# Attention and feed-forward pipeline: the sums of squares moved behind the rotary product, and half of a token shift copied by ScalarE

## The chip, the cores and the metric

The kernel runs on one core of a Trainium2 chip. The metric is the device time of one execution in microseconds (us). The program is static: each engine (TensorE = PE, VectorE = DVE, ScalarE = ACT, GpSimd = POOL) and the DMA-issuing SyncE (SP) has its own instruction list, runs it strictly in order, and meets the others only in semaphores.

## What is computed

The input is x of shape (2, 1024, 128). The output is x + attention(layernorm(x)) + f(layernorm(x)). The first part, 16 causal heads of 8 channels, is not touched by the change. The second part, f, is six layers of:

```
x = attn_layer(shift_tokens(x), ...) + x
x = ffn_layer(shift_tokens(x), ...) + x

def shift_tokens(t):                      # first 64 channels stay, last 64 come from the token before
    a, s = split(t, 2, -1)
    return concatenate([a, pad(s, one row ahead)[:, :-1]], -1)

attn_layer: q, k, v = split(x @ Wqkv)     # 16 heads of 64 channels
    q = q / max(norm(q), 1e-12) * q_scale;  k likewise
    q = q * cos * scale + rotate_half(q) * sin * scale;  k likewise with 1/scale
    windows of 32 queries see 64 keys; softmax(8 * q k^T); out @ Wo
ffn_layer: layernorm(x) * g + b;  a, gate = split(. @ W1 + b1);  (a * gelu(gate)) @ W2 + b2
```

All is float32 in the second part.

## The kernel before

The second part works on tiles of 128 tokens: 6 layers x 16 tiles = 96 tiles (`n_tiles`). It is a software pipeline of 108 steps. In step s each engine runs its share of several tiles at once, in an order written out by hand (loops at L597 for PE, L820 for DVE, L1023 for ACT, L1168 for POOL, L1332 for SP). The feed-forward part handles groups of four tiles and lies 10 steps behind (`FF = 10`). In the text "stage k" is a step s with (s - 10) % 4 = k: normalisation and the two large feed-forward products are started in stage 3, the down product follows in stage 0, the residual and the statistics in stage 1.

For tile n the work is:

- PE `project` (L488) makes q and k (m = 0 and 1) into PSUM, two pairs of banks. ACT `project` (L954) copies both halves into `qk_raw`; ACT squares the copies (L960) into the single buffer `qk_sq`.
- DVE `norms` (L735) sums the squares of 64 channels per head. ACT `roots` (L942 to L946) and POOL `norms` (L1122 to L1130) make the reciprocal norm from it, with one Newton step on POOL.
- DVE `rotate` (L784) multiplies the projection in PSUM with the cosine table into `qk_rot`, one instruction for q and one for k; it waits for ACT's raw copy of the same half. Each releases a pair of PSUM banks (semaphore `rc`). POOL `rotate` makes the sine product out of `qk_raw` (L1151, four instructions) and adds it (L1159, two).
- Two to three steps later DVE `scale` (L743, two instructions) multiplies by the reciprocal norm. PE `turn` (L497) transposes k and q, ACT `turn` copies them out (L967 to L974), PE `score` (L505, L515) makes the window scores, DVE `subtract` (L770 maximum, L774 subtraction) takes the maximum away, ACT `exponents` (L983) exponentiates, DVE `sums` (L757, L759) and `normalise` (L763) divide, PE `weights_turn` (L536) and ACT `weights` (L988) transpose the weights, PE `gather` (L555), ACT `outputs` (L993), PE `output` (L565), DVE `residual` (L752) end the tile. V goes by PE L528, ACT L979, and through DRAM by SP (L1304, L1315).

PSUM is four pairs of banks used in turn; `place` walks the order of use, and each use waits until the reader of the use four places earlier is done. In a step without feed-forward work the order is scores, q, k, output, gather, turned k, turned q, v, turned weights. So turned k of tile s-3 waits for `rotate` of q of tile s, turned q for `rotate` of k of tile s, the gather pair for `subtract`; in stage 3 one more place (normed x turned) makes v wait for ACT `outputs`. The three pairs of the up product (L582), read by `ff_gate` (L806), are reused by q, k and output of the next stage 0.

The engines' orders in one step are:

- PE: score(s-4), project(s), output(s-6), gather(s-5), turn(s-3), [stage 3: L572], project_v(s-2), weights_turn(s-4), [stage 1: shift_in L477], [stage 0: ff_down L592], [stage 3: ff_up L582]
- DVE: scale(s-3), subtract(s-4), [stage 1: ff_residual L817], norms(s-1), rotate(s), residual(s-6), sums and normalise(s-4), [stage 1: ff_stats L796, L798], [stage 3: scale(s-2), which the next step then leaves out, and ff_gate L806]
- ACT: [stage 3: ff_norm L1000], exponents(s-4), project(s) with roots(s-1) and the squares inside it, outputs(s-5), turn(s-3), [stage 3: ff_gain L1008], values(s-2), weights(s-4), [stage 1: shift_in L934, L935], [stage 3: gelu L1018 between two table loads]
- POOL: rotate(s-1), [now and then tables L1085, L1093 and a clearing L1165], [stage 2: ff_rsqrt L1136 to L1141], norms(s-1)

The feed-forward part's own token shift is made by SP in `shift_rows` (L1325 to L1330) in stage 0: three DMAs from `X` to `Xs` (the unshifted 64 channels, 128 KB; the shifted ones, 127 KB; one row), and for the first half of a sequence one more row. `ff_stats` waits for three DMAs of 16 counts each.

Waits are written with `Once`, which leaves out a wait that an earlier one of the same engine covers.

## Time and profile before

| | |
|---|---|
| median of 3 runs | 2046.61 us (2038.38 to 2047.28) |
| the profiled execution, its own time | 2042.86 us |
| span of the profile | 2041.0 us |
| granted TensorE clock, mean | 0.957 of full |
| busy: PE, DVE, ACT, POOL | 92%, 81%, 67%, 68% |
| second part's first projection | at 355 us |
| stage 0 of the first feed-forward group, of the last | at 478 us and 1911.56 us |

The busy share of PE is that of an engine whose matrix products are pipelined and whose ends are modelled. A bracket after a row of the timeline is idle time ahead of it, with the engine and line that released it; "issue" is idle time for which the profile shows no releaser. Times in the timeline are from the start of the span. Durations of POOL are rough; the distance from one start to the next is the better measure.

### The profile page before, as it was taken

To read this page: it belongs to the slowest core of one execution; us is meant where nothing else is said; L and a number is where in the kernel's file an instruction comes from. 1 tells how busy PE (TensorE), PEld (TensorE's weight loads), DVE (VectorE), ACT (ScalarE), POOL (GpSimd) and SP (SyncE) were. 2 spreads that over 40 slices of the span, in tenths; PEclk is the share of its full clock that TensorE was granted. 3 is DMA by queue.
4 is the path that set the end of the run, shared out by engine and by line. 5 is a ranking of instruction groups with operands and counts; after the bars stand their busy time and mean duration, and the time that the engine had idled before them with its cause. 6 is when DMAs were issued, how large, how long until landed. Compare 5 with 4: busy or idle time off the path is not lost.

```text
span 2041.0 us, 73638 instructions
## 1 busy us (share of the span) xinstructions
PE 1872.9 (92%) x32776; PEld 1259.4 (62%) x32776; DVE 1657.3 (81%) x1819; ACT 1373.1 (67%) x2014; POOL 1395.5 (68%) x1277
## 2 busy tenths in 40 slices
PE   3989997889899999999999999999999999999995
PEld 1434443467666766676666676767666766676674
DVE  5777771799798888988888988899878988998872
ACT  1356566677776777776667776777667767777753
POOL 1011112899987889786877788878778878887820
PEclk7689999899999999998999999999999999999997
DMA  3141100254343434444333444344343443333331
GB/s 105 32 142 55 47 25 22 75 134 117 81 120 103 122 101 124 113 116 111 95 107 107 122 115 113 97 112 125 108 112 91 132 121 108 100 96 98 100 101 47
DMA packets 139805, 201.72 MB, mean 99 GB/s; under 512 B 44249, under 2 KB 69085, under 8 KB 138721
## 3 DMA queue, kind: packets, MB, share of 16 engines
q1 hardware_dynamic: 139488, 197.02, 35.0%
q8 instruction: 258, 4.23, 0.9%
q14 instruction: 59, 0.48, 0.1%
HBM read 134.84 MB, written 55.77 MB: 93 GB/s over the span
## 4 chain that ended last, share of the span: by engine, by line
PE 54%; DVE 23%; issue 11%; ACT 6%; POOL 4%; DMA 1%; SPq 0%; DVEq 0%; POOLq 0%; ACTq 0%
PE banks L488 8%; PE banks L582 6%; PE banks L497 5%; PE banks L528 5%; PE banks L515 5%; PE banks L555 4%; PE banks L565 4%; DVE arena L646 4%; DVE ss L735 3%; PE banks L425 3%; PE banks L592 3%; DVE arena L784 3%; PE banks L536 3%; DVE mx_t L770 3%; DVE arena L743 2%
## 5 line engine op out<-in xcount | busy, mean ns | idle before, releaser
L1151 POOL TENSOR_TENSOR arena<-arena,tab_sl 128x512 f32<-128x512 f32 x384 | 600.1, 1594 | 15.7 <-ACT arena L954 8.2
L1159 POOL TENSOR_TENSOR arena<-arena 128x1024 f32<-128x1024 f32 x192 | 493.9, 2593 | 0.0
L743 DVE TENSOR_TENSOR arena<-arena,rn 128x1024 f32<-128x1024 f32 x192 | 379.6, 2017 | 6.8 <-POOL rn L1130 6.4
L488 PE MATMUL banks<-w_qkv,arena 128*128 128x512 f32 x768 | 359.9, 612 | 9.0 <-ACT arena L935 6.6
L983 ACT ACTIVATE arena<-arena 128x1024 f32<-128x1024 f32 x96 | 101.5, 1057 | 360.6 <-DVE arena L774 360.6
L784 DVE TENSOR_TENSOR arena<-banks,tab_cl 128x1024 f32<-128x1024 f32 x192 | 226.2, 1219 | 21.1 <-ACT arena L954 19.3
L488 PEld LDWEIGHTS banks<-w_qkv,arena 128*128 128x128 f32 x768 | 140.2, 192 | 160.9 <-issue 151.4
L646 DVE TENSOR_REDUCE arena<-banks 128x1 f32<-128x512 f32 (+3 forms) x352 | 183.6, 587 | 67.2 <-PE banks L385 55.9
L497 PE MATMUL banks<-ident,arena 128*128 128x128 f32 x1536 | 209.2, 292 | 29.5 <-DVE arena L784 21.3
L1101 POOL TENSOR_SCALAR_AFFINE_SELECT arena<-arena 128x512 f32<-128x512 f32 x64 | 40.9, 640 | 268.6 <-ACT arena L892 268.4
L892 ACT ACTIVATE arena<-banks 128x512 f32<-128x512 f32 (+2 forms) x352 | 156.6, 529 | 101.1 <-PE banks L407 90.8
L735 DVE TENSOR_REDUCE ss<-arena 128x32 f32<-128x2048 f32 x96 | 218.5, 2276 | 1.3 <-ACT arena L960 1.3
L555 PE MATMUL banks<-arena 64*64 64x32 f32 x12288 | 202.5, 220 | 16.6 <-issue 15.2
L565 PEld LDWEIGHTS banks<-w_o,arena 128*128 128x128 f32 x1536 | 189.0, 194 | 45.0 <-issue 33.3
L555 PEld LDWEIGHTS banks<-arena 64*64 64x64 f32 x12288 | 190.6, 135 | 30.7 <-issue 17.4
L497 PEld LDWEIGHTS banks<-ident,arena 128*128 128x128 f32 x1536 | 181.7, 150 | 39.5 <-DVE arena L784 26.8
L528 PE MATMUL banks<-w_qkv,arena 128*128 128x512 f32 x384 | 187.2, 610 | 9.4 <-DVE arena L784 5.5
L954 ACT COPY arena<-banks 128x1024 f32<-128x1024 f32 x192 | 183.9, 1009 | 12.0 <-PE banks L488 7.1
L565 PE MATMUL banks<-w_o,arena 128*128 128x128 f32 x1536 | 190.7, 278 | 1.1 <-ACT arena L993 1.1
L960 ACT ACTIVATE arena<-arena 128x1024 f32<-128x1024 f32 x192 | 191.2, 1044 | 0.0
L770 DVE TENSOR_REDUCE mx_t<-banks 128x16 f32<-128x1024 f32 x96 | 116.7, 1216 | 82.5 <-PE banks L515 82.5
L515 PE MATMUL banks<-arena 64*32 64x64 f32 x12288 | 146.5, 226 | 13.5 <-issue 13.5
(111 smaller groups left out, 3002.9 us busy)
## 6 DMA issues: line engine op xcount, KB each, us to landing
arena<-v_dram SPq DMA_DIRECT2D x360, 256.0 KB, 4.7
v_dram<-arena SPq DMA_DIRECT2D x96, 512.0 KB, 3.1
arena<-parts_dram SPq DMA_DIRECT2D x64, 144.0 KB
w_qkv<-Wqkv SPq DMA_DIRECT2D x6, 1024.0 KB, 5.0
arena<-v_dram SPq DMA_DIRECT2D x24, 192.0 KB, 3.4
parts_dram<-arena SPq DMA_DIRECT2D x12, 256.0 KB, 3.0
tab_cl<-tab_c SPq DMA_DIRECT2D x6, 512.0 KB, 7.7
tab_sl<-tab_s SPq DMA_DIRECT2D x6, 512.0 KB, 10.6
```

The lines of the kernel that those rows point to most:

```text
L488: last = e.matmul(ps[:, BANK * c:BANK * (c + 1)], xsT[b][:, P * t:P * (t + 1)], w_qkv[:, at:at + BANK], start=True, stop=True)
L497: last = e.transpose(ps[:, P * c:P * (c + 1)], qk_rot[n % 4][:, m, P * c:P * (c + 1)], ident)
L515: last = e.matmul(ps[WINDOW * i:WINDOW * (i + 1), col:col + 2 * WINDOW], QT[r, c, WINDOW * i:WINDOW * (i + 1)], KT[n % 2][r, c, WINDOW * i ...
L528: last = e.matmul(ps[:, BANK * hp:BANK * (hp + 1)], xsT[b][:, P * t:P * (t + 1)], w_v[:, hp], start=True, stop=True)
L555: last = e.matmul(ps[d:d + HEAD_DIM, at:at + WINDOW], Vw[n % 3][r, i, P * c + d:P * c + d + HEAD_DIM], PT[r, CHUNKS // 2 * half + c, q], s ...
L565: last = e.matmul(ps[:, 0:P], OT[:, c % 2 * (CHUNKS // 2) + c // 2, :], w_o[l % 2][:, c, :], start=c == 0, stop=c == CHUNKS - 1)
L646: e.tensor_reduce(to, banks[:, pair_of["a_sc", k], BANK * bank:BANK * (bank + 1)].rearrange("p (j n) -> p j n", j=heads.stop - heads.start ...
L735: e.tensor_reduce(ss[n % 4][:, :], qk_sq.rearrange("p m (h d) -> p (m h) d", d=HEAD_DIM), AX_X, ALU.add).then_inc(S["ss_sum"], 1)
L743: e.tensor_tensor(to, to, rn[n % 4][:, HEADS * m:HEADS * (m + 1)].unsqueeze(2).to_broadcast([P, HEADS, HEAD_DIM]), ALU.mult).then_inc(S["r ...
L784: e.tensor_tensor(qk_rot[n % 4][:, m, :].rearrange("p (h d) -> p h d", d=HEAD_DIM), banks[:, pair_of["proj", n, m], :].rearrange("p (h d) ...
L1151: e.tensor_tensor(qk_sw[:, m, :].rearrange("p (h d) -> p h d", d=HEAD_DIM)[:, :, d:d + HALF], raw[:, m, :].rearrange("p (h d) -> p h d", d ...
L1159: e.tensor_tensor(to, to, qk_sw[:, m, :], ALU.add).then_inc(S["rs"], 1)
```

## The change

On DVE, `norms(s-1)` moves from before `rotate(s)` to behind `normalise(s-4)`. On ACT, `project` is split: the copy of q comes ahead of the exponentials; the copy of k stays behind them except in stage 2, where it is ahead too; roots and squares become `squares(s)` and move to the end of the step, ahead of gelu in stage 3. The DMA of the unshifted channels becomes a copy on ACT (`ff_left`, 128 x 256 elements) at the start of stage 0, with a semaphore of its own, and `ff_stats` waits for two DMAs and that copy.

```diff
@@ vector_program @@
             def ff_stats(G):
                 half = G % halves
-                w.wait_ge(xf_in[half], 48 * (G // halves + 1))
+                w.wait_ge(xf_in[half], 32 * (G // halves + 1))
+                w.wait_ge(S["xf_left"], G + 1)
...
-                if 0 <= s - 1 < n_tiles:
-                    norms(s - 1)
                 if s < n_tiles:
                     rotate(s)
...
                     sums(s - 4)
                     normalise(s - 4)
+                if 0 <= s - 1 < n_tiles:
+                    norms(s - 1)
                 if ff_here and k == 1:
                     ff_stats(G)
@@ scalar_program @@
-            def project(n):
-                raw = qk_raw[n % 2]
-                for m in range(2):
-                    w.wait_ge(S["proj"], 2 * n + m + 1)
-                    if n >= 2:
-                        w.wait_ge(S["sw"], 4 * (n - 1))
-                    e.copy(raw[:, m, :], banks[:, pair_of["proj", n, m], :]).then_inc(S["raw"], 1)
+            def project(n, m):
+                w.wait_ge(S["proj"], 2 * n + m + 1)
+                if n >= 2:
+                    w.wait_ge(S["sw"], 4 * (n - 1))
+                e.copy(qk_raw[n % 2][:, m, :], banks[:, pair_of["proj", n, m], :]).then_inc(S["raw"], 1)
+
+            def squares(n):
                 w.wait_ge(S["ss_sum"], n)
                 if n:
                     roots(n - 1)
...
+            def ff_left(G):
+                l, b, half = of_group(G)
+                w.wait_ge(S["x_attn"], GROUP * (G + 1))
+                w.wait_ge(S["xf_norm"], max(0, GROUP * (G - halves + 1)))
+                e.copy(Xs[half][:, :, 0:HEAD_DIM], X[:, b * tiles + half * GROUP:b * tiles + (half + 1) * GROUP, 0:HEAD_DIM]
+                       ).then_inc(S["xf_left"], 1)
...
+                if ff_here and k == 0:
+                    ff_left(G)
                 if ff_here and k == 3:
                     ff_norm(G)
+                if s < n_tiles:
+                    project(s, 0)
+                if s < n_tiles and s >= FF and k == 2:
+                    project(s, 1)
                 if 0 <= s - 4 < n_tiles:
                     exponents(s - 4)
-                if s < n_tiles:
-                    project(s)
-                if s == n_tiles:
-                    roots(s - 1)
+                if s < n_tiles and not (s >= FF and k == 2):
+                    project(s, 1)
...
                     shift_in((s + 1) // GROUP)
+                if s < n_tiles:
+                    squares(s)
+                if s == n_tiles:
+                    roots(s - 1)
                 if ff_here and k == 3:
                     ff_gelu(G)
@@ sync_program, shift_rows @@
-                e.dma_start(to[:, :, 0:HEAD_DIM], xg[:, :, 0:HEAD_DIM]).then_inc(xf_in[half], 16)
```

## Rows read from the trace of the kernel before

**Rows 1.** Busy time by stretch: start:end, length, busy us by engine, clock, DMA share, GB/s
```profile
477.79:1911.56 1433.77, 1371.68 (x26947) 982.00 (x26941) 1257.56 (x1176) 1043.22 (x1428) 1192.95 (x1058) 0.98 0.41 110
```
**Rows 2.** The same columns, stages 0, 1, 2, 3 of one group
```profile
1643.43:1659.75 16.32, 16.32 (x340) 12.80 (x335) 14.16 (x12) 11.28 (x15) 10.14 (x11) 1.00 0.40 104
1659.75:1674.30 14.55, 14.34 (x319) 10.46 (x315) 14.10 (x20) 11.54 (x16) 11.65 (x12) 1.00 0.62 184
1674.30:1690.07 15.77, 14.14 (x311) 9.95 (x311) 15.60 (x12) 10.27 (x14) 13.32 (x14) 1.00 0.31 70
1690.07:1710.21 20.14, 19.73 (x333) 12.58 (x327) 16.70 (x15) 16.36 (x25) 19.53 (x15) 1.00 0.50 140
```
**Rows 3.** Timeline of PE, stages 2 and 3: start us, us, engine line op
```profile
1683.22 2.22 PE L497 MATMUL banks<-ident,arena 128*128 128x128 f32 x16 [1.42 <-DVE arena L784]
...
1700.28 1.98 PE L528 MATMUL banks<-w_qkv,arena 128*128 128x512 f32 x4 [0.39 <-ACT arena L993]
```
**Rows 4.** Waits from 500 to 2000 us: us in total, times, longest
```profile
PE banks L497 <- DVE arena L784: 21.3, 15, 4.6
```
**Rows 5.** Timeline of DVE, starts of stages 1, 2 and 3, and stage 2
```profile
1659.86 1.23 DVE L770 TENSOR_REDUCE mx_t<-banks 128x16 f32<-128x1024 f32 x1 [2.16 <-PE banks L515]
...
1677.21 1.21 DVE L770 TENSOR_REDUCE mx_t<-banks 128x16 f32<-128x1024 f32 x1
...
1679.60 2.27 DVE L735 TENSOR_REDUCE ss<-arena 128x32 f32<-128x2048 f32 x1
1681.94 2.36 DVE L784 TENSOR_TENSOR arena<-banks,tab_cl 128x1024 f32<-128x1024 f32 x2
...
1687.11 4.18 DVE L743 TENSOR_TENSOR arena<-arena,rn 128x1024 f32<-128x1024 f32 x2
1691.21 1.21 DVE L770 TENSOR_REDUCE mx_t<-banks 128x16 f32<-128x1024 f32 x1
```
**Rows 6.** Timeline of PE in an earlier group, stages 2, 3, 0
```profile
1206.04 0.42 PE L555 MATMUL banks<-arena 64*64 64x32 f32 x12 [2.10 <-issue]
...
1214.29 3.70 PE L488 MATMUL banks<-w_qkv,arena 128*128 128x512 f32 x8
...
1233.52 3.70 PE L488 MATMUL banks<-w_qkv,arena 128*128 128x512 f32 x8
...
1245.33 2.84 PE L592 MATMUL banks<-w,arena 128*128 128x128 f32 x24
```
**Rows 7.** Timeline of ACT, stage 3
```profile
1694.68 1.91 ACT L954 COPY arena<-banks 128x1024 f32<-128x1024 f32 x2
...
1697.33 2.00 ACT L960 ACTIVATE arena<-arena 128x1024 f32<-128x1024 f32 x2
...
1704.83 1.28 ACT L1018 ACT_TABLE_LOAD   x1
...
1713.15 1.06 ACT L983 ACTIVATE arena<-arena 128x1024 f32<-128x1024 f32 x1 [1.90 <-DVE arena L774]
```
**Rows 8.** Timeline of DVE, its first work of the next stage 0
```profile
1710.64 1.21 DVE L770 TENSOR_REDUCE mx_t<-banks 128x16 f32<-128x1024 f32 x1
```
**Rows 9.** Timeline of POOL, stages 2 and 3
```profile
1679.58 0.22 POOL L1136 TENSOR_SCALAR ln_v<-mean_var 128x4 f32<-128x4 f32 x1
...
1685.01 7.25 POOL L1151 TENSOR_TENSOR arena<-arena,tab_sl 128x512 f32<-128x512 f32 x4
1692.21 4.68 POOL L1159 TENSOR_TENSOR arena<-arena 128x1024 f32<-128x1024 f32 x2
```
**Rows 10.** Timeline of DVE and POOL past the last tile's rotation
```profile
1952.79 2.42 DVE L743 TENSOR_TENSOR arena<-arena,rn 128x1024 f32<-128x1024 f32 x2
...
1953.12 1.01 POOL L1130 TENSOR_TENSOR rn<-rn,rs_g 128x32 f32<-128x32 f32 x1
```
**Rows 11.** A copy of 128 x 256 on ACT, and the third DMA issue of the shift
```profile
1701.02 0.39 ACT L970 COPY arena<-banks 128x256 f32<-128x256 f32 x1
...
1706.41 8.02 SPq L1327 DMA_DIRECT2D arena<-X  x1
```

More of the change, by code:

```diff
@@ L102 @@
 sc mx sub v_proj v_ready v_out vw_first ex sm recip p_norm pT pt pv ot wo x_attn
-f_stat f_mv f_var f_rstd xf_norm f_nT xft h gel u_one u f_out x_ff final""".split()
+xf_left f_stat f_mv f_var f_rstd xf_norm f_nT xft h gel u_one u f_out x_ff final""".split()
 def build(nc, ins, out, scratch, parts_dram, rows_dram):
@@ L959, in project @@
                     w.wait_ge(S["raw"], 2 * n + m + 1)
-                    e.activation(qk_sq[:, m, :], raw[:, m, :], ACT.Square).then_inc(S["sq"], 1)
+                    e.activation(qk_sq[:, m, :], qk_raw[n % 2][:, m, :], ACT.Square).then_inc(S["sq"], 1)
             def turn(n):
```

## The prediction

> **What bounds the kernel now.** I read the busy time by stretch first. The steady stretch holds 21 feed-forward groups in 1433.8 us, 68.3 us each; PE is busy for 96% of it, DVE 88%, POOL 83%, ACT 73% [rows 1]. So PE is nearly the bound and only its remaining idle time can be won. The same view of one regular group, stage by stage, says where that is: 66.8 us in all, stage 2 being 15.8 us long with 14.1 us of PE [rows 2].
>
> What would PE need undisturbed? Stage 0 shows no wait: 16.3 us [rows 2], of which the down product is 2.8 [rows 6]; a stage without extras is therefore 13.5. Stage 3 without a wait takes 19.2 (the two starts of the projection in an earlier group, [rows 6]), stage 1 has four more transposes, 14.0. The sum, 16.3 + 14.0 + 13.5 + 19.2, is a floor of 63.1 us for a group, 3.7 under the regular one: 2.2 in stage 2, 0.9 in stage 3, 0.5 in stage 1.
>
> The timeline of PE names the waits: in stage 2 turned k waits 1.42 us for the rotary product of DVE, in stage 3 v waits 0.39 us for ACT's `outputs` [rows 3]. The first kind comes back 15 times, 21.3 us in all [rows 4]. The timeline of DVE shows why: it begins stage 2 at 1677.2, 2.9 us behind PE's projection (at 1674.3), because stage 1 took it 17.4 us (1659.9 to 1677.2) [rows 5]. Then the sum of squares runs for 2.3 us, though nobody needs it soon, ahead of the rotary product, which holds the PSUM banks that PE wants [rows 5]. So in stages 1 and 2 DVE ends the wait; in stage 3 the chain comes back through ACT and gelu.
>
> **The change, part by part.** *Sum of squares last on DVE.* No instruction is added or removed. Rotation of q is done 3.6 us after the maximum begins (1.25 + 1.15 for maximum and subtraction, 1.15 for the product) and not after 5.9. PE turns k 7.4 us after its projection began. Before, DVE could be 1.5 us late, now 3.8; the gather wants the subtraction after 5.4 us, and that allows 3.0. With the 2.9 us of stage 2 the whole 2.2 us of stage 2 goes, and the 0.5 of stage 1, whose turned weights come 2.3 us earlier. What is late next: the sum itself, now 9.9 us into DVE's step; ACT's roots wait for it only at the end of the step, after about 13 us. `scale` needs the norm two steps later, so this costs nothing while the roots are where they are.
>
> *Copy of q before the exponentials, squares last on ACT.* Roots and squares (0.8 + 1.9 us, from the end of the copies to the end of L960 [rows 7]) stood ahead of `outputs`; without them `outputs` starts at once when the gather ends, and the 0.9 us of stage 3 goes. Against it:
> (a) In stages 0, 1 and 3 the copy of k stays behind the exponentials. It is ready 1.06 + 0.95 us [rows 7] after the subtraction, but DVE is through with q after 1.15: a new wait of 0.9 us in three stages, 2.7 a group, that the sum of squares used to cover.
> (b) In stage 3 the 2.7 us now stand ahead of the table load. Gelu used to be ready for stage 0 to begin on DVE 5.8 us after the load began (1704.8 to 1710.6 [rows 7, 8]); DVE's stage 0 will now begin about 3 us after PE's projection and not 0.4. Maximum and subtraction are then done at 5.5 us (wanted 5.4), rotated k at 8.9 (8.3), weights at about 11.8 (10.9): about 0.8 us of PE waits in stage 0 and 0.3 in stage 3.
> ACT itself has room, 49.5 of 66.8 us busy [rows 2].
>
> *POOL.* The roots reach POOL some 9 us later in a step, so its norms and the next rotation move by as much. Its work is 54.6 of 66.8 us [rows 2], and its result is used two steps on, so nothing waits for the rotation. One thing may: `ff_rsqrt`, which ran at 1679.6, over 10 us before stage 3 began at 1690.1 [rows 9, 2]. One rotation is 7.2 + 4.7 us [rows 9]; put behind the later roots, it ends some 2.8 us into stage 3, while ACT would take `ff_norm` at 2.1. That holds the copy of q there by about 2.3 us, but DVE, itself late by then, loses only 0.3.
>
> *Does DVE become the bound?* Its loop, from the rows: stage 0 14.0, stage 1 17.4, stage 2 14.0 (1677.2 to 1691.2), stage 3 to the end of the sum 9.8, then roots and squares 2.7, and 5.8 from table load to stage 0 [rows 5, 7, 8]: 63.7, and 2.7 with (a): 66.4 us, hardly less than now. But `scale` is not one size. Beside POOL's large products its two instructions take 4.18 us [rows 5]; after the last rotation, beside small POOL work, they take 2.42, and a POOL instruction of a quarter of a us takes 1.01 beside them [rows 10]. The later roots leave POOL idle or in its small operations just when DVE scales in stages 0 and 1. I price this between 0 (same overlap) and 4 x 1.76 = 7.0 us a group (never beside a large product), and take two stages, 3.5 us: the loop is 62.9 and PE bounds again. I take the nearer value since POOL is still busy for 55 of 64 us and must overlap elsewhere.
> The Trainium skill (SBUF — State Buffer, Who interferes with whom) states that a DVE instruction with two SBUF inputs and a GpSimd one that reads SBUF exclude each other, the second one blocking fully; by it `scale` would pay for every large POOL product in progress and nothing beside a waiting POOL. It would make the sum depend on POOL's phase alone, as taken above, not on its busy share.
>
> *The DMA replaced.* Removed: 24 DMAs of 128 KB and their SP issues; the third issue of the shift, behind them, takes 8.0 us [rows 11], so SP may reach the V windows sooner, but these are wanted two steps later and no PE wait on them is seen. Added: 24 copies of 128 x 256 at 0.39 us [rows 11], 9 us of ACT. They lie after the second table load of stage 0, where ACT now idles 1.9 us before the exponentials [rows 7]; with gelu 2.7 us later that cover is gone for the copy of q, yet DVE's subtraction ends later still, so I cost it at 0; uncovered it would be 0.4 x 21 = 8 us. `ff_stats` needs the data some 25 us later: nothing. Behind the DMA, no gain either; bounds: 0, and the instruction stalls below if they come from DMA load.
>
> *Start and end.* In the first ten steps POOL's rotation sets the pace and is unchanged; in the last ten steps no projection is left. I take 0, between -5 and +5.
>
> *The sum.* A regular group becomes 17.1 (stage 0) + 14.0 + 13.5 + 19.5 = 64.2, that is 2.6 us less; 21 of them, 54 us. PE also has stalls with no releaser, such as 2.10 us within the gather [rows 6]; about 30 us in the stretch. Today half of that falls into time in which PE would wait for DVE anyway; it comes into the open and gives 15 us back. 2042.9 (the profiled execution's own time, 1.9 above its span and 3.7 under the median of the three runs) - 39 is 2003.9. Against the median that is 2007; I take 2004, as a faster run lies at 2038.
>
> **The rivals.** A difference of 0.5%, 10 us, is about what a measurement of this kernel can tell from no change.
> *Bigger gain.* `scale` is freed in all stages, so the new waits vanish too: the group comes to its floor, 3.7 x 21 = 77 us, about 1968. For it: the late POOL phase. Against: POOL's large products must lie somewhere. 0.15.
> *Nothing much.* The overlap stays as it is, and (a) replaces the sum of squares as what DVE stands on: 66.4 against 66.8 us, 8 us in all, 2036. For it: 4.18 us of `scale` in nearly every step today. 0.14. That the reorder doesn't free the banks I exclude: each rotation releases them itself.
> *Slower, by `ff_rsqrt`.* If POOL gets no relief, a rotation takes 13.9 and not 11.9, and `ff_norm`, first in ACT's stage 3, waits until 4.7 us into it. Copy of q, rotation, sum of squares, roots and gelu shift in a row, about 2 us on a loop of 66.4: 68.4 against 66.8, and 1.6 x 21 = 34 us, 2076 (2050 if half of it is absorbed). It decides from the point at which `ff_rsqrt` ends later than about 3 us into stage 3. Against it: today 10 us of room. 0.14.
> *The forecast*, 1985 to 2030: 0.57.
>
> **The numbers.** The range leaves out the far ends of the bigger gain and of the slower case: 1966 to 2052. Faster by over 0.5% is the forecast, the bigger gain and a small part of the third case: 0.73; within 0.5% 0.13; slower 0.14.
>
> **What would show it.** In the changed profile: the wait of L497 for DVE L784 near zero and stage 2 at 13.5 us; v in stage 3 without a wait; about 0.9 us of DVE idle time before the second L784 released by ACT's copy in stages 0, 1 and 3; gelu 2 to 3 us later; `scale` nearer 2.4 than 4.2 us in stages 0 and 1; POOL's wait for the roots now at the end of a step. Wrong would be: waits of L515 or L555 for DVE L774 or L784 of over 1 us a group, of ACT L1000 for POOL L1141, or stage 0 over 17.5 us.

## The result, and the profile after

| | before | after |
|---|---|---|
| median | 2039.95 us (6 runs, 2037.17 to 2047.28) | 2025.79 us (6 runs, 2020.29 to 2033.02) |
| profiled execution | 2042.86 us, span 2041.0 | 2033.02 us, span 2031.2 |
| first stage 0 of the feed-forward, last | 477.8, 1911.56 us | 484.21, 1900.63 us |
| 21 groups between them | 1433.8 us | 1416.4 us |

The ratio is 0.9933, 95% interval 0.9914 to 0.9952: faster by 0.67%, where 2.1% was forecast (2004 against the median of 2046.61 us known then). The range of 1966 to 2052 us holds it. The two spans differ by 9.8 us: 6.4 us lost before the first group, 17.4 us won in the steady stretch, 1.1 us lost behind it.

Busy time by stretch, after: stages 0 to 3 of one group, then all 21 groups (columns as in [rows 1]).
```profile
1495.89:1512.87 16.98, 16.73 (x341) 12.70 (x335) 13.49 (x13) 13.78 (x18) 8.06 (x8) 1.00 0.38 101
1512.87:1527.15 14.28, 14.14 (x320) 10.53 (x315) 13.30 (x18) 9.17 (x12) 12.30 (x8) 1.00 0.42 112
1527.15:1541.35 14.20, 13.82 (x311) 9.99 (x311) 14.10 (x13) 11.52 (x16) 13.42 (x12) 1.00 0.44 114
1541.35:1562.00 20.65, 19.70 (x331) 12.61 (x327) 16.48 (x14) 17.27 (x26) 19.59 (x21) 1.00 0.30 83
484.21:1900.63 1416.42, 1359.71 (x26946) 971.07 (x26940) 1186.60 (x1174) 1082.63 (x1450) 1097.42 (x1052) 0.99 0.40 109
```
Against [rows 2] stage 2 is 1.6 us shorter, but stage 0 is 0.7 us longer and stage 3 0.5: 66.1 us a group instead of 66.8, where 64.2 was forecast.

PE is busy for nearly all of this, and yet it is not what sets the 66.1 us. In another group of the changed kernel, stages 2 and 3 read:
```profile
985.93:1001.58 15.65, 14.05 (x310) 10.06 (x310) 15.55 (x14) 12.94 (x19) 14.79 (x13) 1.00 0.39 105
1001.58:1020.81 19.23, 19.23 (x328) 12.46 (x326) 15.12 (x13) 15.67 (x23) 18.25 (x20) 1.00 0.29 86
```
```profile
1001.39 0.27 PE L515 MATMUL banks<-arena 64*32 64x64 f32 x2 [1.22 <-issue]
```
A stall of PE (1.22 us idle, no releaser) makes stage 2 about 1.4 us longer here, stage 3 is shorter by as much, and the group takes 66.1 us again (16.98 + 14.28 + 15.65 + 19.23). Ten of the 21 groups lie between 66.10 and 66.24 us, however their stages are divided; they are called regular below, and undisturbed where PE has no stall either. Before, eight lie between 66.74 and 66.78 us. So a chain that runs through the other engines too sets the length, and it leaves PE about 1.4 us of slack in these two stages.

DVE and POOL are busy for 71 and 96 us less than in [rows 1]: that relief is real, but most of it doesn't reach PE. DVE's waits for ACT's copies, below, grow by 70 us.

The waits from 500 to 2000 us, after (us in total, times, longest), against [rows 4]:
```profile
POOL ss L1138 <- ACT rn L943: 277.0, 62, 9.0
DVE arena L784 <- ACT arena L953: 78.1, 86, 2.1
PE banks L536 <- DVE arena L763: 14.2, 22, 2.6
ACT arena L1008 <- POOL ln_m L1157: 12.9, 14, 2.8
PE banks L497 <- DVE arena L784: 1.1, 4, 0.3
```
The wait of turned k (L497) is gone, as forecast: 21.3 to 1.1 us. In its place stand more waits of DVE for ACT's copies (before: 7.7 us, 3 times), of PE for the normalised weights (before: 5.1 us, 14 times) and of ACT's `ff_norm` for POOL.

The timeline of DVE in stage 3, after (start us, us, engine line op; in brackets the idle time ahead):
```profile
1542.84 1.21 DVE L770 TENSOR_REDUCE mx_t<-banks 128x16 f32<-128x1024 f32 x1
1544.09 1.23 DVE L774 TENSOR_TENSOR arena<-banks,mx_t 128x1024 f32<-128x1024 f32 x1
1547.12 1.23 DVE L784 TENSOR_TENSOR arena<-banks,tab_cl 128x1024 f32<-128x1024 f32 x1 [1.80 <-ACT arena L953]
1548.87 1.23 DVE L784 TENSOR_TENSOR arena<-banks,tab_cl 128x1024 f32<-128x1024 f32 x1 [0.53 <-ACT arena L953]
...
1551.74 2.22 DVE L763 TENSOR_TENSOR arena<-arena,rs_o 128x1024 f32<-128x1024 f32 x1
1553.89 2.27 DVE L735 TENSOR_REDUCE ss<-arena 128x32 f32<-128x2048 f32 x1
```
What it waits for stands in ACT's timeline of the same stage:
```profile
1544.44 1.65 ACT L1008 ACTIVATE arena<-arena,ln_m,ln_r 128x128 f32<-128x128 f32 x4 [0.93 <-POOL ln_m L1157]
1546.00 0.99 ACT L953 COPY arena<-banks 128x1024 f32<-128x1024 f32 x1
```
and what follows, in PE's:
```profile
1554.11 1.07 PE L536 MATMUL banks<-ident,arena 128*128 128x128 f32 x8 [0.44 <-DVE arena L763]
```
`ff_norm` stands in ACT's list ahead of the copy of q, and waits for the last instruction of POOL's `ff_rsqrt`, which now follows a rotation that the later roots have shifted. The copy of q stands behind both that wait (0.93 us) and `ff_norm` itself (1.65 us):
```profile
1535.01 5.68 POOL L1175 TENSOR_TENSOR arena<-arena 128x1024 f32<-128x1024 f32 x2
...
1544.21 0.20 POOL L1157 TENSOR_TENSOR ln_m<-ln_m,ln_r 128x4 f32<-128x4 f32 x1
```
DVE stands still for 2.3 us (1.80 + 0.53), so sum, division and turned weights come late.

The groups of instructions of DVE and POOL from 500 to 1900 us (count | busy us, mean ns of one): first before, then after.
```profile
L743 DVE TENSOR_TENSOR arena<-arena,rn 128x1024 f32<-128x1024 f32 x164 | 329.5, 2049 | 0.2 <-issue 0.2
L763 DVE TENSOR_TENSOR arena<-arena,rs_o 128x1024 f32<-128x1024 f32 x82 | 116.0, 1415 | 2.8
L1151 POOL TENSOR_TENSOR arena<-arena,tab_sl 128x512 f32<-128x512 f32 x332 | 517.5, 1590 | 6.5
```
```profile
L743 DVE TENSOR_TENSOR arena<-arena,rn 128x1024 f32<-128x1024 f32 x167 | 199.9, 1236 | 0.0
L763 DVE TENSOR_TENSOR arena<-arena,rs_o 128x1024 f32<-128x1024 f32 x83 | 174.5, 2102 | 2.9
L1167 POOL TENSOR_TENSOR arena<-arena,tab_sl 128x512 f32<-128x512 f32 x334 | 357.9, 1104 | 6.6
```
`scale` (L743) costs 130 us less in all, more than the 3.5 x 21 = 74 us forecast, and POOL's sine products 160 us less. But `normalise` (L763), which lay clear of the large products and now lies beside POOL's addition, costs 58 us more, and that one stands directly ahead of PE's L536. This fits the rule of the Trainium skill weighed in the prediction (SBUF — State Buffer, Who interferes with whom): a DVE instruction with two SBUF inputs and a GpSimd one that reads SBUF exclude each other. The trace agrees: `scale` and `normalise` both have two SBUF inputs, and each is long where it lies beside one of POOL's products or additions. Below this is called the lock of the two engines.

### The profile page after: what moved, and what is told of

It reads as the page before. It is cut to its first block, busy times and chain, and to the rows that moved or that the text cites. A ratio compares the mean times of both kernels' runs of the same rounds, so it can differ in the third digit from the quotient of the medians.

```text
span 2031.2 us, 73684 instructions
## 1 busy us (share of the span) xinstructions
PE 1864.3 (92%) x32776; PEld 1253.0 (62%) x32776; DVE 1591.5 (78%) x1819; ACT 1415.4 (70%) x2038; POOL 1305.3 (64%) x1277
## 4 chain that ended last, share of the span: by engine, by line
PE 48%; DVE 21%; ACT 15%; issue 10%; POOL 5%; DMA 1%; SPq 0%; DVEq 0%; ACTq 0%; POOLq 0%
PE banks L488 8%; PE banks L497 5%; PE banks L555 4%; PE banks L582 4%; PE banks L528 4%; PE banks L565 4%; DVE arena L646 4%; PE banks L425 3%; DVE arena L763 3%; PE banks L592 3%; PE banks L515 3%; PE banks L536 3%; ACT arena L953 3%; DVE sm_t L757 3%; ACT arena L1026 2%
## 5 line engine op out<-in xcount | busy, mean ns | idle before, releaser
L1175 POOL TENSOR_TENSOR arena<-arena 128x1024 f32<-128x1024 f32 x192 | 499.1, 2624 | 0.0
L1167 POOL TENSOR_TENSOR arena<-arena,tab_sl 128x512 f32<-128x512 f32 x384 | 414.3, 1112 | 15.7 <-ACT arena L953 8.2
L784 DVE TENSOR_TENSOR arena<-banks,tab_cl 128x1024 f32<-128x1024 f32 x192 | 232.7, 1221 | 100.7 <-ACT arena L953 100.5
L1138 POOL TENSOR_SCALAR ss<-ss 128x32 f32<-128x32 f32 x96 | 69.2, 721 | 284.5 <-ACT rn L943 281.8
L743 DVE TENSOR_TENSOR arena<-arena,rn 128x1024 f32<-128x1024 f32 x192 | 244.1, 1311 | 0.0
L953 ACT COPY arena<-banks 128x1024 f32<-128x1024 f32 x192 | 192.0, 1004 | 63.7 <-PE banks L488 63.1
L497 PE MATMUL banks<-ident,arena 128*128 128x128 f32 x1536 | 209.7, 290 | 19.9 <-issue 12.6
L994 ACT COPY arena<-banks 128x1024 f32<-128x1024 f32 x96 | 97.4, 1015 | 156.6 <-PE banks L555 156.3
L763 DVE TENSOR_TENSOR arena<-arena,rs_o 128x1024 f32<-128x1024 f32 x96 | 198.4, 2067 | 3.3
L497 PEld LDWEIGHTS banks<-ident,arena 128*128 128x128 f32 x1536 | 178.6, 148 | 33.0 <-issue 19.9
L961 ACT ACTIVATE arena<-arena 128x1024 f32<-128x1024 f32 x192 | 190.9, 1042 | 0.0
```

The source lines that it names most:

```text
L497: last = e.transpose(ps[:, P * c:P * (c + 1)], qk_rot[n % 4][:, m, P * c:P * (c + 1)], ident)
L743: e.tensor_tensor(to, to, rn[n % 4][:, HEADS * m:HEADS * (m + 1)].unsqueeze(2).to_broadcast([P, HEADS, HEAD_DIM]), ALU.mult).then_inc(S["r ...
L763: e.tensor_tensor(PB, PB, rs_o[n % 2][:, :].unsqueeze(2).to_broadcast([P, HEADS, 2 * WINDOW]), ALU.mult).then_inc(S["p_norm"], 1)
L784: e.tensor_tensor(qk_rot[n % 4][:, m, :].rearrange("p (h d) -> p h d", d=HEAD_DIM), banks[:, pair_of["proj", n, m], :].rearrange("p (h d) ...
L953: e.copy(qk_raw[n % 2][:, m, :], banks[:, pair_of["proj", n, m], :]).then_inc(S["raw"], 1)
L1167: e.tensor_tensor(qk_sw[:, m, :].rearrange("p (h d) -> p h d", d=HEAD_DIM)[:, :, d:d + HALF], raw[:, m, :].rearrange("p (h d) -> p h d", d ...
```

## The experiments

All profiled runs are read alike; T is the start of the first stage 0, "steady" the 21 groups behind it, the stages are medians in us. Ratios are to the kernel before, measured together with the run. T, steady and the stages come from one profile each: before and e1 have the same regular groups (66.8 us), and their steady stretches still differ by 6 us. A difference of that size in this column is no finding; the length of the regular groups repeats to 0.1 us.

| run | ratio (95%) | T | steady | st. 0 | st. 1 | st. 2 | st. 3 |
|---|---|---|---|---|---|---|---|
| before | | 477.8 | 1433.8 | 16.32 | 14.55 | 15.77 | 20.14 |
| after | 0.9933 (0.9914-0.9952) | 484.2 | 1416.4 | 17.01 | 14.30 | 15.62 | 19.78 |
| e1 | 0.9976 (0.9960-0.9992) | 476.4 | 1427.8 | 16.32 | 14.55 | 15.77 | 20.14 |
| e2 | 0.9942 (0.9919-0.9966) | 484.6 | 1409.1 | 17.01 | 14.29 | 15.21 | 19.66 |
| e3 | 0.9947 (0.9928-0.9967) | 486.4 | 1417.8 | 17.01 | 14.29 | 14.83 | 20.21 |
| e4 | 0.9920 (0.9892-0.9948) | 477.5 | 1418.0 | 17.01 | 14.29 | 15.31 | 19.77 |
| e5 | 0.9896 (0.9848-0.9945) | 486.8 | 1402.0 | 16.43 | 14.29 | 15.97 | 19.79 |
| e6 | 1991.05 us, one run | 474.0 | 1387.7 | 16.98 | 14.28 | 14.66 | 19.23 |
| e7 | 0.9826 (0.9810-0.9843) | 479.4 | 1392.4 | 16.32 | 14.29 | 14.76 | 19.60 |
| e8 | 2025.54 us, one run | 472.5 | 1425.0 | 16.32 | 14.55 | 15.77 | 20.14 |
| e9 | 2010.43 us, one run | 480.4 | 1396.5 | 17.01 | 14.29 | 14.20 | 20.68 |
| e10 | 0.9880 (0.9859-0.9901) | 474.8 | 1404.8 | 16.43 | 14.29 | 15.65 | 19.89 |
| e13 | 1997.48 us, one run | 467.3 | 1401.2 | 16.32 | 14.55 | 15.22 | 19.79 |
| e14 | 0.9878 (0.9839-0.9917) | 481.6 | 1395.6 | 16.99 | 14.29 | 15.42 | 19.23 |
| e15 | 0.9771 (0.9732-0.9810) | 475.9 | 1377.4 | 16.32 | 14.29 | 14.26 | 19.23 |
| e16 | 0.9846 (0.9814-0.9879) | 480.5 | 1397.9 | 16.40 | 14.29 | 15.29 | 19.23 |

### The parts of the change, each alone

e1 is the kernel before with `ff_left` and its waits, and without the first DMA of the shift (the changed waits of `ff_stats` are as in the change):
```diff
+                if ff_here and k == 0:
+                    ff_left(G)
...
-                e.dma_start(to[:, :, 0:HEAD_DIM], xg[:, :, 0:HEAD_DIM]).then_inc(xf_in[half], 16)
```

> The kernel before with only the DMA of the unshifted channels replaced by the ScalarE copy; the orders of VectorE and ScalarE as before. Theory A (the copy and the DMA are both hidden; the result comes from the two orders alone): within 0.3% of the kernel before, stage 0 stays at 16.3 us, stage 2 at 15.8. Rival B (fewer small DMA packets relieve PE's instruction stalls): 0.3 to 0.8% faster, and idle time of PE before L555, L515 and L497 put down to issue falls from about 32 us to under 20. Rival C (the copy delays stage 0): stage 0 at 16.6 us or more, 0.3% slower.

e2 is the changed kernel with that DMA back:
```diff
-                w.wait_ge(xf_in[half], 32 * (G // halves + 1))
-                w.wait_ge(S["xf_left"], G + 1)
+                w.wait_ge(xf_in[half], 48 * (G // halves + 1))
...
+                e.dma_start(to[:, :, 0:HEAD_DIM], xg[:, :, 0:HEAD_DIM]).then_inc(xf_in[half], 16)
```


> The changed kernel with the DMA restored and the ScalarE copy taken out; both new orders stay. Theory A: the same as the changed kernel within 0.3% (ratio to before about 0.993), stage 0 at 17.0 us. Rival C (the 0.4 us copy at the head of stage 0 costs): 0.2 to 0.4% faster than the changed kernel, stage 0 at 16.6 us. Rival B: slower than the changed kernel by 0.3% or more, with more issue stalls.

Theory A of both runs holds. The copy alone is worth 0.24%, the order alone 0.58%; all regular stages of e1 are those of before to 0.01 us. With the change's 0.67% the parts about add up, but with intervals of 0.2 to 0.25% that is all these two can say. The 0.24% lies below the size of Rival B and above none at all; stalls of PE without a releaser are 25.7 us in e1 and 30.4 before. That the copy on ACT costs nothing, as forecast, is what the stages show.

e11 moves only the sum of squares on DVE, ACT as before.
```diff
-                if 0 <= s - 1 < n_tiles:
-                    norms(s - 1)
                 if s < n_tiles:
                     rotate(s)
...
                     normalise(s - 4)
+                if 0 <= s - 1 < n_tiles:
+                    norms(s - 1)
```


> The kernel before with only the sum of squares on VectorE moved behind the normalisation; ScalarE's order stays, so roots and squares still stand ahead of its outputs and wait for the sum. Theory A (the move needs the other one: ScalarE stops until 10 us into VectorE's step, and outputs, turned k and q come some 4 to 5 us late): 3 to 8% slower than before. Rival K (ScalarE's slack absorbs the wait): within 1% of before.

2598.93 us in one run, 27% more; Theory A had the direction, and with 3 to 8% far too small a size. The waits of e11, 500 to 2600 us:
```profile
ACT rn L942 <- DVE ss L735: 585.8, 88, 7.0
DVE mx_t L770 <- PE banks L515: 432.6, 68, 9.6
PE banks L536 <- ACT arena L993: 305.7, 67, 5.2
```
ACT's roots and squares, still ahead of `outputs`, wait for a sum that now comes last: both moves are one.

### The start

e4 keeps both old orders in the first ten steps and takes the new ones from step 10 on (the part on DVE; ACT's list is split at `FF` in the same way).
```diff
+                if 0 <= s - 1 < n_tiles and s < FF:
+                    norms(s - 1)
                 if s < n_tiles:
                     rotate(s)
...
-                if 0 <= s - 1 < n_tiles:
+                if 0 <= s - 1 < n_tiles and s >= FF:
                     norms(s - 1)
...
```


> The changed kernel with the old orders of VectorE and ScalarE in steps 0 to 9, before the first feed-forward group, and the new ones from step 10 on. Theory A (the first stage 0 came 6.4 us later than before, since in the fill GpSimd's additions lie beside the scaling and lengthen it): the first stage 0 at 478 us again and not 484, 5 to 6 us faster than the changed kernel, ratio to before about 0.990. Rival E (the later start is chance: an instruction stall of 2.5 us with a slow clock after it lies there): the first stage 0 stays at 482 or later, under 2 us gained.

T returns to 477.5 us, the steady stretch stays (1418.0), and Theory A holds. So the new order itself costs these 6 us. The other profiles agree: the five with the changed kernel's first steps (after, e2, e3, e5, e14) have T at 481.6 to 486.8 us, the four with the old ones (before, e1, e4, e10) at 474.8 to 477.8. `scale` in the first steps, first in the changed kernel, then in e4:
```profile
378.71 6.25 DVE L743 TENSOR_TENSOR arena<-arena,rn 128x1024 f32<-128x1024 f32 x2
...
419.79 5.56 DVE L743 TENSOR_TENSOR arena<-arena,rn 128x1024 f32<-128x1024 f32 x2
```
```profile
400.96 3.26 DVE L743 TENSOR_TENSOR arena<-arena,rn 128x1024 f32<-128x1024 f32 x2 [0.86 <-POOL rn L1154]
414.55 3.28 DVE L743 TENSOR_TENSOR arena<-arena,rn 128x1024 f32<-128x1024 f32 x2
```
In a step without feed-forward work `scale` has moved onto POOL's large products: the opposite of the steady stretch.

### The waits of stages 0 and 3

e3 puts POOL's `ff_rsqrt` ahead of its norms and rotation in stage 2.
```diff
+                if s >= FF and k == 2 and G < n_groups:
+                    ff_rsqrt(G)
...
-                if s >= FF and k == 2 and G < n_groups:
-                    ff_rsqrt(G)
```

> The changed kernel, and on GpSimd in stage 2 ff_rsqrt ahead of the rotation and not behind it. Theory A (the later roots push ff_rsqrt behind the start of stage 3, and that makes the copy of q, the weights and gelu late): ScalarE's wait at L1008 for GpSimd (12.9 us, 14 times) goes, stage 3 falls from 20.7 to 19.9 us in regular groups, 8 to 15 us faster than the changed kernel, ratio to before about 0.987. Rival D (what ends stage 3 late is the normalisation slowed beside GpSimd's addition, and the gelu chain): the wait goes but stage 3 stays above 20.4 us, and the time changes by less than 4 us.

`ff_norm` no longer waits (its 12.9 us are gone), yet steady is 1417.8: Theory A falls, and the outcome is Rival D's, though by another way. POOL's phase has moved: the `scale` just ahead of DVE's stage 3 takes 4.51 us where it took 2.34, DVE begins that stage 3.6 us behind PE and not 1.5, and the gather waits for `subtract` (4.1 us in all). In an undisturbed group stage 2 is down to 13.8 us and stage 3 up to 21.15: the same sum.

e5 puts squares and roots behind gelu in stage 3, e10 is e4 and e5 together.
```diff
+                if ff_here and k == 3:
+                    ff_gelu(G)
+                    e.preload_act_table_set(ACT_SET)
                 if s < n_tiles:
                     squares(s)
                 if s == n_tiles:
                     roots(s - 1)
-                if ff_here and k == 3:
-                    ff_gelu(G)
-                    e.preload_act_table_set(ACT_SET)
```


> The changed kernel with roots and squares of stage 3 behind gelu on ScalarE and not ahead of it. Theory A (roots and squares ahead of gelu delay VectorE's start of stage 0, and PE loses there what stage 0 grew by, from 16.3 to 17.0 us): stage 0 back at 16.3 to 16.5, 8 to 14 us faster than the changed kernel, ratio to before 0.987 to 0.990. Rival F (the later roots only move the delay to stage 1, since the sum and the scaling come later): stage 0 near 16.4 but stage 1 or 2 longer by as much, under 4 us gained.

> The changed kernel with both mends: the old orders in steps 0 to 9, and from step 10 on roots and squares behind gelu in stage 3. If the two are independent, as theory A has it (6 us in the fill, 13 us from stage 0): first stage 0 at 478 us, stage 0 at 16.4, ratio to before 0.985 to 0.988, faster than either kernel. Rival: instruction stalls take part of it, ratio 0.989 or more.

Stage 0 falls from 17.01 to 16.43 us and the steady stretch by 14.4 us, as Theory A of e5 has it. The ratio goes to 0.9896, but its interval overlaps that of the changed kernel, so the time alone doesn't settle it. With the old start it is 0.9880, at the upper end of what was expected.

e7 copies k ahead of the exponentials in every stage.
```diff
-                if s < n_tiles and s >= FF and k == 2:
+                if s < n_tiles:
                     project(s, 1)
                 if 0 <= s - 4 < n_tiles:
                     exponents(s - 4)
-                if s < n_tiles and not (s >= FF and k == 2):
-                    project(s, 1)
```


> The changed kernel with the copy of k ahead of the exponentials in every stage and not in stage 2 alone. Theory A (VectorE's wait of 0.5 to 0.9 us for the copy of k in stages 0, 1 and 3 is not what PE waits for, since the weights wait for GpSimd's lock): stages change by under 0.3 us each, time within 0.4% of the changed kernel. Rival J (that wait delays the normalisation and with it L536): the 78 us of VectorE's waits at L784 fall below 40, stage 3 falls by 0.5 us, 6 to 10 us faster than the changed kernel.

Theory A falls: the one line gives 1.1% on top of the change, 24 us in the steady stretch. Rival J has the direction, but none of its numbers: the total of DVE's wait for ACT's copies goes from 78.1 to 46.4 us and not below 40, the gain is more than twice its 6 to 10 us, and the undisturbed stage 3, 20.66 us, has not moved. What moves is stage 0, to 16.32, what it was before, and the undisturbed stage 2, 14.2 to 13.9: a regular group takes 65.2 us. e5 and e7 each bring stage 0 back by themselves, which looks like two lateness terms that add in DVE and of which PE feels only what exceeds its slack.

e14 leaves e7's edit out and moves `ff_norm` behind both copies.
```diff
-                if ff_here and k == 3:
-                    ff_norm(G)
                 if s < n_tiles:
                     project(s, 0)
...
+                if ff_here and k == 3:
+                    ff_norm(G)
                 if 0 <= s - 5 < n_tiles:
                     outputs(s - 5)
```


> The changed kernel with ACT's `ff_norm` of stage 3 issued behind the exponentials and both copies, ahead of `outputs` (it stood ahead of everything). Nothing is left out. In the changed kernel a regular stage 3 takes 20.7 us, 1.45 above the 19.2 it needs; there `ff_norm` waits 0.92 us for POOL, and DVE waits 1.80 us for the copy of q behind it. Theory M (the copy of q behind `ff_norm` is what holds stage 3): that wait of DVE goes to under 0.5 us and a regular stage 3 becomes 19.3 to 19.8, so 21 stages give 19 to 29 us on the steady stretch, against which at most 0.4 us a group is lost where `outputs` starts after `ff_norm`: 8 to 25 us faster than the changed kernel, ratio to the kernel before 0.981 to 0.989. Rival N (the slowed normalisation of q and k, 2.1 to 2.9 us beside POOL's additions, is the longer of two chains): the wait of DVE goes, but stage 3 stays at 20.3 or above, and the ratio at 0.991 to 0.995. Rival O: `ff_norm` beside or behind the exponentials delays the feed-forward transposes of the same stage, and stage 3 rises above 21.

Stage 3 of e14 (columns as above), and DVE in it:
```profile
1523.81:1543.29 19.48, 19.48 (x334) 12.71 (x327) 16.73 (x14) 17.15 (x26) 18.66 (x18) 1.00 0.32 87
```
```profile
1527.71 1.22 DVE L784 TENSOR_TENSOR arena<-banks,tab_cl 128x1024 f32<-128x1024 f32 x1
1529.83 1.23 DVE L784 TENSOR_TENSOR arena<-banks,tab_cl 128x1024 f32<-128x1024 f32 x1 [0.90 <-ACT arena L953]
...
1532.70 1.46 DVE L763 TENSOR_TENSOR arena<-arena,rs_o 128x1024 f32<-128x1024 f32 x1
```
The wait of 1.80 us is gone, PE works through the whole stage, and 19.23 us, the floor of the prediction, is the median. Theory M holds: the steady stretch is 20.8 us shorter than after, the ratio 0.9878, and groups without a stall take 64.7 to 65.0 us where they took 66.1. Against e3, which took away only the 0.93 us of waiting and won nothing, e14 also takes the 1.65 us of `ff_norm` from ahead of the copy of q. `normalise` of stage 3 is shorter here too (1.46 us shown; in the median of the stages 3 1.47 against 2.25), so up to 0.8 us a group may come by way of the rival's cause; e14 doesn't separate the two.

e15 has the edits of e7 and e14:
```diff
-                if ff_here and k == 3:
-                    ff_norm(G)
                 if s < n_tiles:
                     project(s, 0)
-                if s < n_tiles and s >= FF and k == 2:
+                if s < n_tiles:
                     project(s, 1)
                 if 0 <= s - 4 < n_tiles:
                     exponents(s - 4)
-                if s < n_tiles and not (s >= FF and k == 2):
-                    project(s, 1)
+                if ff_here and k == 3:
+                    ff_norm(G)
```
e16 has e5's in addition.

> Both edits together: the copy of k ahead of the exponentials in every stage and `ff_norm` of stage 3 behind them. Nothing is left out. The copy of k alone brought the ratio to the kernel before to 0.9826, with stage 3 at 20.7 us where it ran undisturbed. Theory M: the gains add up, stage 3 goes to 19.3 to 19.8 in this one too, 10 to 25 us off 2002.8: ratio 0.970 to 0.978. Rival N: 0.980 to 0.985, stage 3 at 20.3 or above.

> As the one before, and squares and roots of stage 3 also behind the gelu. Nothing is left out. In the changed kernel gelu ahead of them gave 0.2 to 0.4% by itself, through stage 0 (17.0 to 16.4 us); with the copy of k early stage 0 is at 16.3 already. Theory M: no more than 5 us to either side of the one before, since stage 0 has nothing left to win. Rival P: gelu late still delays DVE in stage 0 by more than shows there, and its later stages win: 8 to 15 us faster than the one before. Rival Q: the roots, later still, push POOL's rotation onto the next stage's scaling: over 8 us slower.

e15 is the fastest kernel here: 1989.70 us in the median of 4 runs, 2.3% under the kernel before (1.9 to 2.7) and about 1.7% under the changed one (1.8% by the medians, 1.6% by the two ratios). Theory M holds here too. One of its groups and the steady stretch:
```profile
1259.44:1276.57 17.13, 16.51 (x341) 12.71 (x335) 14.53 (x13) 13.73 (x18) 13.63 (x18) 1.00 0.45 118
1276.57:1290.86 14.29, 14.15 (x321) 10.54 (x315) 13.45 (x18) 9.29 (x12) 9.02 (x7) 1.00 0.30 77
1290.86:1305.08 14.22, 13.79 (x310) 9.96 (x311) 14.12 (x13) 11.49 (x16) 13.44 (x12) 1.00 0.71 191
1305.08:1324.31 19.23, 19.23 (x333) 12.52 (x327) 17.61 (x14) 17.13 (x26) 18.01 (x21) 1.00 0.33 88
475.90:1853.30 1377.40, 1341.79 (x26946) 966.99 (x26940) 1219.36 (x1174) 1079.36 (x1451) 1100.17 (x1050) 1.00 0.41 112
```
Its undisturbed groups take 63.7 us (16.32 + 14.29 + 13.90 + 19.23), a little under the 64.2 that the prediction gave for the change.

e16 is 17 us slower than e15, as Rival Q had it in size. Its cause doesn't show: the `scale` of the next stage 1 is not longer than in e15. What stands out is a new wait of DVE in stage 0 of e16:
```profile
1351.53 2.36 DVE L784 TENSOR_TENSOR arena<-banks,tab_cl 128x1024 f32<-128x1024 f32 x2 [2.31 <-ACT arena L953]
```
Roots and squares, put behind gelu and the second table load, stand ahead of the copy of q of stage 0. But that wait is no loss by itself: e5 has it as well (2.3 us in the median, 46 us in all in both runs), DVE begins stage 0 2.7 us earlier in e16 than in e15, and the median of stage 0 grows by only 0.08 us. The loss lies in stage 2 (15.29 against 14.26 us), where PE's stalls without a releaser are 9 us more in the gather. The order that came out well in e5 hurts once the copies are early; why stays open.

### POOL's additions and the V windows

e6 (the changed kernel) and e13 (the kernel before) let POOL add 128 of 1024 columns only.
```diff
-                    e.tensor_tensor(to, to, qk_sw[:, m, :], ALU.add).then_inc(S["rs"], 1)
+                    e.tensor_tensor(to[:, 0:P], to[:, 0:P], qk_sw[:, m, 0:P], ALU.add).then_inc(S["rs"], 1)
```


> The changed kernel with GpSimd's two additions of the sine product on 128 of 1024 columns only, so that most of the sine part is left out of q and k. Theory A (the normalisation takes 2.1 us and not 1.25 because it now lies beside these additions): L763 back at 1.25 us, the waits of L536 for L763 gone, stage 2 at 13.6 us where no instruction stall lies in it, no wait of L1008 for GpSimd; the steady stretch 8 to 15 us shorter. Rival G (the normalisation is no bound; PE's instruction stalls are): L763 at 1.25 us and yet the steady stretch changes by less than 4 us.

> The kernel before with GpSimd's two additions on 128 of 1024 columns, so that most of the sine part is left out, the pair to the same cut of the changed kernel (steady stretch 1387.7 us). Theory D (in the changed kernel the additions hold up the normalisation, in the one before they lie beside little that PE waits for): the steady stretch falls by under 20 us from 1433.8, to 1415 to 1434, so that without the additions the change is worth 30 to 45 us and not 17. Rival L (the additions cost both kernels alike): it falls by 25 to 35 us, to about 1402, and the change stays worth about 17 us.

Without the additions `normalise` is back at 1229 ns, stage 3 at 19.23 and the changed kernel's steady stretch 28.7 us shorter. But the kernel before gains as much by the same cut (1433.8 to 1401.2, 32.6 us). So Rival L holds, and Theory D falls: with the additions cut the change is worth 13.5 us of the steady stretch, with them 17.4. In the changed kernel the additions do hold the group (the undisturbed one falls from 66.1 to 64.1 us), but they hold the one before as much (66.8 to 64.9), so their cost is not what the change added.

e8 (before) and e9 (after) load 64 of 512 columns of each V window from the fourth tile on.
```diff
-                        e.dma_start(Vw[n % 3][r:r + WINDOW, first:WPT, :], rows[:, :, BANK * hp:BANK * (hp + 1)]).then_inc(vw_in[n % 3], 16)
+                        cols = BANK if n < 3 else 64
+                        e.dma_start(Vw[n % 3][r:r + WINDOW, first:WPT, 0:cols], rows[:, :, BANK * hp:BANK * hp + cols]).then_inc(vw_in[n % 3], 16)
```

> The kernel before with the loads of the V windows cut to 64 of 512 columns from the fourth tile on, so that the attention gathers stale values. Theory H (PE's idle time put down to issue comes from the refill of its instructions behind these loads): issue stalls of PE in the steady stretch fall from 30 us to under 8; since half of them lie in time in which PE waits for VectorE anyway, the stretch gets only about 15 us shorter. Rival I (refill stalls have nothing to do with these loads): issue stalls stay near 30 us.

> The changed kernel with the same cut of the V window loads. Theory H: issue stalls fall from 40 us to under 8, and as they are not covered any more the steady stretch gets 35 to 45 us shorter, 1375 to 1382 us; against the kernel before with the same cut the change is then worth 35 us or more. Rival I: issue stalls near 40 us, stretch near 1416.

Stalls of PE without a releaser fall from 30.4 to 10.6 us before and from 39.5 to 10.7 us after; more stays than was expected (under 8), but Theory H stands in the main and Rival I falls. The steady stretches gain less than Theory H had: 8.8 us and not 15 before, 19.9 us and not 35 to 45 after, and between e8 and e9 the change is worth 28.5 us and not 35. e9 shows what a group of the changed kernel is when PE has no stall: 17.01 + 14.28 + 14.20 + 20.68 = 66.2, no shorter than the groups of the changed kernel that read 17.0, 14.3, 15.6 and 19.2, with a stall in stage 2. Taking a stall out doesn't shorten a regular group, since PE doesn't set its length.

## Why the prediction was right or wrong

**Right: the first half of the mechanism.** The wait of L497 went from 21.3 to 1.1 us; stage 0 came to 17.01 us (17.1 said); in stage 0 DVE waits 0.89 us for the copy of k (0.9 said), in stages 1 and 3 0.53; v waits for nothing in stage 3; the roots reach POOL late, and `scale` is short; the DMA replaced cost nothing.

**Wrong: the size**, 17.4 us in the steady stretch where 39 were summed, and with it the sentence "the loop is 62.9 and PE bounds again". That the time lies in the stated range owes more to its width than to the sum. The prediction had DVE's loop through a group at 62.9 us, shorter than PE's 64. It can be read off where DVE begins each stage with the maximum, and where ACT begins the table load:
```profile
1498.72 1.21 DVE L770 TENSOR_REDUCE mx_t<-banks 128x16 f32<-128x1024 f32 x1
...
1512.98 1.23 DVE L770 TENSOR_REDUCE mx_t<-banks 128x16 f32<-128x1024 f32 x1 [1.19 <-PE banks L515]
...
1529.45 1.21 DVE L770 TENSOR_REDUCE mx_t<-banks 128x16 f32<-128x1024 f32 x1
```
```profile
1559.04 1.28 ACT L1026 ACT_TABLE_LOAD   x1
```
```profile
1564.85 1.21 DVE L770 TENSOR_REDUCE mx_t<-banks 128x16 f32<-128x1024 f32 x1
```
With 1542.84 for stage 3 the loop is 66.1 us, as long as the group: this chain, in which PE has only a part, sets the pace. Stages 0 to 2 take 44.1 us of it, 0.4 over the prediction's terms with its relief of `scale`. Stage 3 to the end of the sum takes 13.3 us where 9.8 and the 0.9 of (a) were counted: 2.6 us too little, of the 3.2 in all. Two things make up most of it: waits of 2.33 us instead of 0.9, and `normalise`, 2.22 us instead of 1.23. The term of stage 3 is the step that failed. The terms by stage, against a regular group:

- *Stage 3, 19.5 said, 20.65 found: 1.15 x 21 = 24 us.* `ff_rsqrt` was to end 2.8 us into the stage, and ends 3.1 us into it (1544.41 against 1541.35): right. Then came "DVE, itself late by then, loses only 0.3". For that it would have to be some 2.7 us behind PE; it is 1.5 behind (1542.84 against 1541.35), and was 1.1 behind in [rows 2, 5] as well. The 2.9 us that the prediction had in mind are those of stage 2. So DVE loses 1.80 us for q and 0.53 for k. e14 takes `ff_norm` out of the way and gives 20.8 us back. A wait of ACT's `ff_norm` for POOL was among the prediction's own signs of being wrong, and it came (12.9 us, 14 times). The rival of `ff_rsqrt` had its place right and its size too large; the rival that had DVE's loop at 66.4 us came nearest in length, but by luck: it had `scale` unrelieved.
- *Stage 2, 13.5 said, 14.2 found: 15 us.* The 13.5 was 0.1 low: the shortest stage 2 that e6 shows is 13.61. The wait of L497 left, but the one behind it, of L536 for `normalise`, was not priced. Here the lock of the two engines does reach PE:
```profile
1535.83 2.62 DVE L763 TENSOR_TENSOR arena<-arena,rs_o 128x1024 f32<-128x1024 f32 x1
...
1538.60 1.06 PE L536 MATMUL banks<-ident,arena 128*128 128x128 f32 x8 [0.38 <-DVE arena L763]
```
- *Stage 1, 14.0 said, 14.28 found: 6 us.* The term was too low: 13.61 us and the transposes of L477 (0.53) make 14.14. The rest is a wait of the next projection for ACT's `shift_in`, which ends at 1527.01; PE goes on at 1527.15.
- *Stage 0* is 0.1 us better than said, 2 us. In sum the four terms, 64.1 us and not 64.2 as the prediction adds them up (its floor, too, adds up to 63.0 and not 63.1), are 2.0 us a group or 43 us too low. Against the regular group before, 66.8, the change wins 0.6 us, 13 us in 21 groups.
- *Stalls, 15 us to be lost.* They grew (30.4 to 39.5 us in the steady stretch), but this term rests on PE as the bound, and a part of them falls into the slack: what all groups take beyond the regular length is 32 us before and 27 us after. Those 4 to 5 us and the 13 make the 17.4 measured. In e15 the same excess is 40 us (1377.4 against 21 x 63.7), with 26.6 us of stalls.
- *The clock, not in the sum.* Stretches at 1.2 GHz add up to 58 us before and 27 us after (granted in the mean 0.98 and 0.99), and PE's busy time is 12 us less for the same instructions. How much of this reaches the time, and how much of it belongs to the change and not to one profiled execution, isn't settled.
- *Start, 0 with a bound of 5 said, 6.4 us found.* "POOL's rotation sets the pace and is unchanged" left out that `scale` would now run beside it; e4 shows it.

That `scale` would be relieved by more than two stages' worth, 130 us against 74, is what the bigger gain needed; it did not follow, as waits on ACT took the place. Not tried: e15 with the old orders in the first steps, where T, at 475.9 us, leaves little to win; and a run that shortens only stage 3's `normalise`, which would say how much of the 20.8 us of e14 is its share.

## What to carry to other kernels

A busy share of 96% doesn't make an engine the bound: look whether a stall of it lengthens the period at all. Lateness that is to cover a new wait is a number of one stage: read it in the stage where the wait will stand, and then price the next wait behind it too. In each engine's list, put what releases another engine (here a PSUM copy) ahead of what waits for a third one or is used later (here a normalisation). Look at each reorder again when the others are in: the same late squares came out 0.4% faster alone (within the noise of the time, though not of the stages) and cost 0.8% in company.

## What the runs showed of the hardware

- **The lock moves, it doesn't go.** A pair of `scale` takes 2.35 us clear of POOL's large products and mostly 4.2 to 4.5, at most 6.4, beside them; `normalise` 1.23 clear and in the steady stretch up to 2.9 beside an addition. Where the DVE instruction wins, POOL pays: its 128 x 32 operations, 0.24 to 0.33 us, take about 1 us beside `scale`:
```profile
1527.44 1.13 POOL L1138 TENSOR_SCALAR ss<-ss 128x32 f32<-128x32 f32 x1 [2.20 <-ACT rn L943]
1528.65 0.98 POOL L1140 TENSOR_TENSOR rs_g<-rn 128x32 f32<-128x32 f32 x1
1529.71 0.25 POOL L1142 TENSOR_TENSOR rs_g<-rs_g,ss 128x32 f32<-128x32 f32 x1
```
- **PE's stalls without a releaser follow DMA load.** Cutting the V windows' bytes by seven eighths (110 to 57 GB/s over the steady stretch) took away two thirds of them or more, in either order of work (one profile each; in the other runs, e11 aside, they are 25.7 to 39.5 us). The profile doesn't show what PE waits for in them.
